# A two-layer macaron transformer kernel: layer norm, router and combine weights of the first MoE chunk move one chunk up, and the key copies are cleared at the beginning

## The reference

```python
x = x + 0.5 * ffn0(layernorm(x))        # FFN0: its own layer norm, 128 -> 512, silu, 512 -> 128
x = x + linear_attention(layernorm(x))  # LIN: 16 heads, plus a local convolution
x = x + 0.5 * ffn0(layernorm(x))        # FFN1: the same weights
x = x + 0.5 * moe(layernorm(x))         # MOE0
x = x + causal_attention(layernorm(x))  # CAUSAL: 16 heads of 8, rotary positions
x = x + 0.5 * moe(layernorm(x))         # MOE1
```

```python
logits = x @ router_w.T                     # 16 experts
top_w, top_i = top_k(softmax(logits), 2); top_w = top_w / sum(top_w)
h = silu(x @ Wg[e]) * (x @ Wu[e])           # for every expert e, 64 wide
out = sum over e of dense_w[:, e] * (h @ Wd[e])
out = out + sigmoid(x @ shared_gate_w) * ((silu(x @ Sg) * (x @ Su)) @ Sd)
```

## Time and profile before

| what | value |
|---|---|
| median of 3 runs | 713.02 us (710.68 to 713.17) |
| the profiled execution | 713.36 us, span 711.6 us |
| PE busy | 630.4 us, 89% |
| DVE busy | 491.2 us, 69% |
| ACT busy | 357.0 us, 50% |
| POOL busy | 162.9 us, 23% |

### The profile page before, as it was taken

One profiled execution on the slowest core, in us unless ns is written; L12 is line 12 of the kernel. 1 busy time (PEld: TensorE's weight loads), 2 busy tenths in 40 slices (PEclk: granted clock), 3 DMA queues, 4 the chain that ended last, 5 costly groups with the idle time before them and its releaser, 6 DMA issues.

```text
span 711.6 us, 11849 instructions
## 1 busy us (share of the span) xinstructions
PE 630.4 (89%) x4028; PEld 459.5 (65%) x4028; DVE 491.2 (69%) x1528; ACT 357.0 (50%) x727; POOL 162.9 (23%) x290
## 2 busy tenths in 40 slices
PE   1877677969999987799998989999999998999998
PEld 1756566858887975465555555555656554788887
DVE  3568883755877759977765657787887831777765
ACT  3744335312323464166668767666566676332221
POOL 4573354250003540001524240112211000100000
PEclk9999979969999995789999999999999999999999
DMA  7000000032232200000000000000000000333342
GB/s 271 1 1 1 1 0 1 1 120 82 100 118 68 87 29 0 1 1 1 1 1 1 0 1 1 2 0 1 2 1 1 1 2 16 105 110 105 117 136 75
DMA packets 18667, 27.88 MB, mean 39 GB/s; under 512 B 2984, under 2 KB 7208, under 8 KB 18608
## 3 DMA queue, kind: packets, MB, share of 16 engines
q1 hardware_dynamic: 17888, 25.85, 11.1%
q10 hardware_dynamic: 720, 1.28, 0.5%
HBM read 25.79 MB, written 1.33 MB: 38 GB/s over the span
## 4 chain that ended last, share of the span: by engine, by line
PE 68%; DVE 12%; ACT 3%; issue 3%; POOL 3%; DMA 1%; SPq 0%; DVEq 0%; POOLq 0%
PE bank L1583 12%; PE bank L1611 10%; PE bank L1541 10%; PE bank L1481 9%; PE bank L1271 6%; PE bank L1273 6%; PE bank L1272 6%; PE bank L1593 2%; DVE hn L882 2%; DVE bank L1154 1%; DVE work L1157 1%; PE bank L1551 1%; PE bank L1510 1%; PE bank L1522 1%; PE bank L1279 1%
## 5 line engine op out<-in xcount | busy, mean ns | idle before, releaser
L791 ACT ACTIVATE arena<-bank 128x512 f32<-128x512 f32 (+3 forms) x384 | 166.9, 493 | 88.2 <-PE bank L1593 64.8
L1154 DVE CUSTOM_DVE_ANT_0 bank<-bank,mask_qk 128x512 f32<-128x512 f32 (+3 forms) x256 | 121.1, 512 | 47.6 <-PE bank L1611 46.6
L1611 PE MATMUL bank<-kza,qta 128*128 128x512 f32 (+3 forms) x320 | 126.5, 409 | 4.9 <-DVE work L1154 1.3
L1583 PE MATMUL bank<-qtb,kza 128*128 128x512 f32 (+3 forms) x320 | 120.1, 387 | 2.0 <-DVE work L1154 1.0
L718 ACT ACTIVATE work<-bank 128x512 f32<-128x512 f32 x80 | 47.7, 598 | 121.0 <-PE bank L1273 115.6
L1157 DVE TENSOR_REDUCE work<-bank 128x1 f32<-128x512 f32 x128 | 81.6, 684 | 24.4 <-PE bank L1611 23.8
L1583 PEld LDWEIGHTS bank<-qtb,kza 128*128 128x128 f32 x320 | 60.4, 191 | 57.5 <-ACT arena L791 51.6
L1481 PE MATMUL bank<-dw,work 128*128 128x128 f32 x640 | 87.1, 281 | 6.1 <-DVE work L1084 6.1
L1481 PEld LDWEIGHTS bank<-dw,work 128*128 128x128 f32 x640 | 83.5, 196 | 10.4 <-issue 6.3
L1080 DVE TENSOR_TENSOR work<-work,bank 128x512 f32<-128x512 f32 x80 | 54.9, 686 | 50.7 <-PE bank L1273 45.9
L1541 PE MATMUL bank<-arena 128*9 128x512 f32 (+3 forms) x768 | 79.9, 488 | 0.4 <-ACT arena L791 0.4
(11 more groups left out here) (193 smaller groups left out, 1149.0 us busy)
## 6 DMA issues: line engine op xcount, KB each, us to landing
kt<-cw_rows SPq DMA_DIRECT2D x160, 128.0 KB, 2.9
x<-x_in SPq DMA_DIRECT2D x4, 256.0 KB, 8.8
y_out<-x SPq DMA_DIRECT2D x4, 256.0 KB, 3.1
arena<-gw_in SPq DMA_DIRECT2D x1, 640.0 KB, 8.8
arena<-uw_in SPq DMA_DIRECT2D x1, 640.0 KB, 8.4
dw<-dw_in SPq DMA_DIRECT2D x1, 640.0 KB, 9.4
work<-q_in SPq DMA_DIRECT2D x2, 256.0 KB, 6.6
arena<-wa_in ACTq DMA_DIRECT2D x1, 393.0 KB, 7.0
```

What stands on the lines that cost most here:

```text
L791: act.activation(pb[:, blk % 2, h, 0:w], s_bank(n)[:, 0:w], ACT.Exp, scale=SCALE).then_inc(p_ready, 1)
L1154: ins = dve.tensor_tensor_reduce(out=src, in0=src, in1=mask_qk[:, CW - w:], scale=1.0, scalar=-3e38, op0=ALU.add, op1=ALU.max, accum_out=dst)
L1583: ins = pe.matmul(s_bank(n)[:, 0:w], kz(s, h, j // CT)[:, j % CT * P:(j % CT + 1) * P], qtb[:, s % 2, (c + 1) * CW - w:(c + 1) * CW], star ...
L1611: pe.matmul(a_bank(n)[:, 0:w], qta[:, slot(b, g), i * P:(i + 1) * P], kz(s, h, half)[:, 0:w], start=True, stop=True).then_inc(a_full, 1)
```

## The change

TensorE: in FFN1 `ln(12)` moves from behind gate product 13 to behind gate product 11; `route` from behind gate product 15 to behind gate product 13; `weights(0)` from behind the second gate and up pair of MOE0 to between down products 14 and 15 of FFN1. ScalarE's order follows. VectorE: `split(12)` moves from the last chunk's turn to the one before, `weigh(0)` now stands ahead of `update(11)`. GpSimd: the four clears move from behind `rstd(14)` to the kernel's beginning, ahead of `rstd(0)`.

```diff
@@ gpsimd
             pool.memset(nhalf[:, :], -0.5)
+            pool.memset(stm[:, :, :, :, :].bitcast(F32), 0.0)
+            for z in kza:
+                pool.memset(z[:, :, :].bitcast(F32), 0.0)
             rstd(0)
...
-                if L == 14:
-
-                    pool.memset(stm[:, :, :, :, :].bitcast(F32), 0.0)
-                    for z in kza:
-                        pool.memset(z[:, :, :].bitcast(F32), 0.0)
@@ scalar, ffn
-                    if k == 1:
+                    if k == 1 and m < 28:
                         ln(4 * p + n // FB + 1)
+                    if m == 27:
+                        ln(4 * MOE0)
+                    if m == 30:
+                        route(0)
...
                 if p == FFN1:
-                    route(0)
+                    weights(0)
@@ scalar, moe
-                if p == MOE0:
-                    weights(r0)
@@ vector, ffn
-                    split(L + 1)
+                    if L + 1 < 4 * MOE0:
+                        split(L + 1)
                     norm(L + 2)
+                    if L + 2 == 4 * MOE0:
+                        split(L + 2)
                     if L + 1 == 4 * MOE0:
                         route(0)
+                        weigh(0)
                     update(L, 0.25)
-                    if L + 1 == 4 * MOE0:
-                        weigh(0)
                     moments(L + 3)
@@ tensor, ffn
-                        if k == 1:
+                        if k == 1 and m < 28:
                             ln(4 * p + c + 1)
-                        if n == NC * FB - 1 and p == FFN1:
+                        if m == 27:
+                            ln(4 * MOE0)
+                        if m == 29:
                             route(4 * MOE0, 0)
+                    if n == NC * FB + 1 and p == FFN1:
+                        weights(0)
```

## The result

The changed kernel took 718.53 us (median of 4, 718.04 to 718.96) against 713.1 for the kernel before (4 runs, 710.68 to 714.55): ratio 1.0081, 95% interval 1.0055 to 1.0108. It is slower by 0.8%, 5.4 us; 713.3 and "no change" had been forecast, the range ended at 718.0. On a second chip it was 1.0076 (1.0050 to 1.0103).

The account below looks back on a forecast made before the run. TensorE, busy 89% of the span, was taken as the bound. Later product +2.8, clock behind it -4.8, clock at the new hole +0.95, beginning +1.3 gave +0.25: 713.6 on the profiled scale, 713.3 against the median; range 710 to 718.

Parts of the forecast that it names:

- clock behind it -4.8: Behind MOE0's first expert product: the 12.3 us at half clock go, -6.2, of which -4.8 us stays as VectorE becomes last.
- The later product (+2.8): End of FFN1: the weights' transposes, and with them MOE0's first expert product, come 2.8 us later.
- stall at chunk 12's transposes: FFN1, behind gate product 11: TensorE stands still 3.47 us for VectorE's normalisations; 3.2 us of filling work comes later.
- route ahead of down product 11: FFN1: the route's 1.36 us moves ahead of down product 11, so VectorE's update of chunk 10 slips 4.56 us in all.
- VectorE's queue: Behind update 10, moments and normalisation 13, search and weigh follow, ending at 145.0; TensorE idles 4 us before the weights' transposes.
- The clock at the new hole (+0.95, an even chance of 1.9): Before chunk 12's transposes: the 3.47 us hole may lower TensorE's clock, costing 1.9 us at even odds, 0.95 on average.
- Behind the product: At full clock VectorE is last: second chunk's weights 11.5 us after the first expert product, TensorE arrives at 10.2.
- The beginning (+1.3): Kernel's start: the clears delay the first reciprocal root and VectorE's first normalisation, +1.3 us, bounds 0 and 1.85.
- The delay of the root: Kernel's start: GpSimd's clears last until 7.06, so the first reciprocal root slips 1.85 us from 5.21.
- The clears taken out of the MoE (0): MoE's start: removing the clears there gains 0, since nothing waits for GpSimd there.
- Rival 1: Before the first expert product the half clock stays, so the -4.8 is not won: 718.1 us, chance 0.17.

Follow-up runs that it names:

- before_again: The kernel before, without edit, measured and profiled once more: 712.14 us, ratio 1.0023.
- clears_only: The kernel before with only the four clears moved to the beginning: 714.42 us, ratio 1.0027.
- before_warm: The kernel before plus matmuls whose results nobody reads, ahead of chunk 11's transposes and of MOE0's first expert product: 713.1 us, ratio 0.9996.
- search_first: The kernel before, but search and weigh ahead of normalisation 13 and update 11, weights' transposes ahead of the first gate and up pair: 710.73 us, ratio 0.9972.
- moves_route_back: moves_only with the route put back behind gate product 15: 716.18 us, ratio 1.0053.
- early_ln: The kernel before with only chunk 12's transposes and split moved up, TensorE's behind gate product 11: 716.11 us, ratio 1.0041.
- late_only: The kernel before with only weigh ahead of update 11 and the weights' transposes between down products 14 and 15: 711.59 us, ratio 0.9980.
- moves_search_first: moves_only, but search and weigh right behind split 12, ahead of update 10, and weights' transposes behind gate product 14: 715.69 us, ratio 1.0032.
- moves_only: The changed kernel with the four clears put back behind the reciprocal root of L = 14: 719.96 us, ratio 1.0111; again 718.66 us, ratio 1.0053.

## Why the prediction was wrong

Order and place of every wait up to the first expert product came out as forecast; the failed step is the term "clock behind it -4.8" of the sum.

- **The gain behind the first expert product (-4.8): mis-sized, and this decides.** It was half of a half-clock stretch of 12.3 us read from one profile. Against that profile it holds nearly: from the product to update 12 the change took 25.63 instead of 29.76, -4.1. But the two other profiles with the same order there (before_again, clears_only) took 26.27 and 26.15. Against them the gain of the change is 0.5 to 0.6, against the mean of the three profiles 1.8. And before_warm, where all this half clock is gone, was not faster in the time; its interval leaves 2.0 us at most. So the term is -0.5 to -1.8 and not -4.8. I took one draw for a property. A short stretch costs little there: the 4.9 us at half clock behind the product of before_again (151.40 to 156.3) cost 0.7 (26.27 against 25.57 in before_warm) and not 2.5, because at full clock TensorE waits 1.19 for VectorE ahead of the second weights' transposes anyway. The draw was not a rare one: of seven profiles in which the clock fell around this product with its hole unfilled, three have the long stretch (before, search_first, moves_route_back: 28.9 to 29.8) and four the short one (before_again, clears_only, early_ln, late_only: 25.6 to 26.6). That the stretch can be short was readable from the first profile: behind chunk 11's transposes the clock was back inside 3.5 us.
- **The later product (+2.8).** To the weights +2.24 and to the product +0.3 with filled holes: right. Its parts, stall at chunk 12's transposes, route ahead of down product 11, VectorE's queue, were each shown (early_ln, moves_route_back, moves_search_first).
- **The clock at the new hole (+0.95, an even chance of 1.9).** In the four profiles of the change and of moves_only it fell each time and cost 1.6 (15.3 instead of 13.69), once 2.8. In three other kernels with that hole (early_ln, moves_route_back, moves_search_first) it did not fall. The price was right; whether the odds were too, four of four against none of three does not tell.
- **Behind the product** VectorE became the last, as forecast: 1.20 us idle ahead of the second weights' transposes (11.5 - 10.2 = 1.3 had been worked out).
- **The beginning (+1.3): the size about right, by luck.** The delay of the root was right (6.99 against 7.06), and so was the 0.6 of the first normalisation (0.62 to 0.88 in three profiles). The second half, that the normalisation is shut out by GpSimd's two small operations, was wrong; in its place came 0.7 to 1.0 by update 1, where the clock fell near 39. Together about 1.4 at the end of FFN0.
- **The clears taken out of the MoE (0).** Nothing waited for them in the kernel before, but with the moves and the clears left there VectorE's split did (1.33 to 2.80 instead of 0.42 in five kernels). The two halves of the change depend on each other, and the prediction weighed them one by one.
- **Together:** the steps as measured give +2.5 (later product) + 1.6 (clock at the hole) - 0.6 (behind it, against the short stretch) + 1.4 (beginning) = 4.9; against the mean of the three profiles 3.7, against the long one 1.4. Measured were 5.4, interval 3.9 to 7.7. The two runs of moves_only, 1.0111 and 1.0053, have intervals that do not meet; this stays open.

Rival 1, the half clock that stays, had the right size (718.1) for the wrong reason: the clock did come back before the expert product; what was missing was most of the gain behind it.

## What to carry to other kernels

A stretch at half clock that follows a hole is worth what it is in several executions, not what one profile shows: before a gain is booked on it, look at the spread of the times, and take a second profile. When a chain is moved up, look at what stands ahead of it in the in-order queue of the slowest consumer: moving the search and weigh ahead of work that nobody waits for shortened the stretch by 1.5 to 2.2 us (0.3% in the time, with an interval that reaches 1), moving the inputs ahead of work that was ready cost 0.4%. Moving an instruction ahead of ready work is free only if its inputs are ready at that place too. And when work moves, look at what now runs beside it on the other engines: clears that disturbed nobody held up a VectorE copy once the chain around them had shifted.

## What the runs showed of the hardware that was not expected

The same GpSimd addition of 128x512 (1.27 us) that stretched a VectorE normalisation from 1.11 to 2.07 did so by holding up one of its four instructions (1.30 instead of 0.34), while GpSimd's scalar operation and copy of 128x128 (0.57 and 0.31) beside the first normalisation held up none (0.341 to 0.347 each, in three profiles). GpSimd's clears of 128x2048 (1.8 each) held up a VectorE copy of 128x512 that came while one ran, in five kernels, until 0.27 to 0.29 us after the end of that clear or of the next. So the rule of the Trainium skill quoted in the prediction (page SBUF - State Buffer, the part on its two sides), that the loser of the shared ports blocks for a whole instruction, agrees with the addition and the clears and not with the two small operations, which by it should have held the normalisation up. The same part of the Trainium skill limits it to VectorE instructions in a two-port mode or, against a GpSimd instruction that reads SBUF, with two inputs there, but the VectorE instruction beside the addition and beside the two small operations is the same.

And one binary spreads over 9 us (708.7 to 717.5 in 35 executions). The two profiles of the kernel before agree within 0.1 us up to the first place where the clock falls differently. Those of moves_only are 0.80 apart at the first update already: the kernel's first 128x512 matmuls take 0.63 instead of 0.40, and this lasted until 22.3 us in one and until 25.4 in the other.
